# A 16-block attention and mixture-of-experts kernel on one core: q and the output projection as float32r parts, k stored once and read back three times, and new places for all steps

## The reference, cut to what matters

```python
def xattn(q, ctx, w_q, w_kv, w_concat):          # 16 heads of 16, one k and one v shared by all heads
    qh = (q @ w_q).reshape(B, L, 16, 16)
    k, v = split(ctx @ w_kv)
    p = softmax(qh k^T / 4)                       # per block of 128 rows
    return (p v).reshape(B, L, 256) @ w_concat
x = x + xattn(layernorm(x), ctx, ...)
a = layer_norm(layernorm(x)) * nw + nb            # 2048 rows
expert, place = top-1 gate of a, 8 experts, 256 places each
moe = gate * (gelu(a[expert rows] @ W1[e] + b1) @ W2[e] + b2)       # 256 -> 1024 -> 256
res = gelu(a @ R1 + rb1) @ R2 + rb2               # a dense layer of the same shape for all rows
out = x' + coef0 * res + coef1 * moe              # x' = layernorm(x)
```

## Time and profile before

| | us |
|---|---|
| median of 3 runs | 365.86 (365.32 to 366.06) |
| the profiled execution: its own time | 366.06 |
| its span in the profile | 364.3 |
| PE busy | 323.8, 89% of the span |
| DVE, ACT, POOL busy | 228.4, 242.6, 159.8 |
| TensorE's mean granted clock | 0.936 of full |

### The profile page before, as it was taken

One profiled execution on the slowest core, in us unless ns is written; L12 is line 12 of the kernel. 1 busy time (PEld: TensorE's weight loads), 2 busy tenths in 40 slices (PEclk: granted clock), 3 DMA queues, 4 the chain that ended last, 5 costly groups with the idle time before them and its releaser, 6 DMA issues.

```text
span 364.3 us, 7025 instructions
## 1 busy us (share of the span) xinstructions
PE 323.8 (89%) x2514; PEld 280.4 (77%) x2514; DVE 228.4 (63%) x577; ACT 242.6 (67%) x439; POOL 159.8 (44%) x219
## 2 busy tenths in 40 slices
PE   3765887998999999899999989998899999999990
PEld 2543543877897798698798776898899999999990
DVE  4225546985576676576675765465577987788630
ACT  3222277694287588388587476687699999999650
POOL 4222124426986575655654652638003332133222
PEclk9955589996999999999999999999899999999996
DMA  6395756625105505503405301941489888971122
GB/s 186 117 251 160 226 151 175 183 65 161 52 30 180 138 1 173 131 4 122 121 8 166 75 17 38 337 161 40 139 260 318 235 251 266 211 235 21 19 25 29
DMA packets 52490, 49.87 MB, mean 137 GB/s; under 512 B 6684, under 2 KB 49640, under 8 KB 52456
## 3 DMA queue, kind: packets, MB, share of 16 engines
q1 hardware_dynamic: 49384, 45.22, 41.8%
q0 software_dynamic: 3072, 4.21, 6.2%
HBM read 33.65 MB, written 15.63 MB: 135 GB/s over the span
## 4 chain that ended last, share of the span: by engine, by line
PE 73%; DMA 6%; DVE 6%; ACT 5%; POOL 4%; issue 3%; SPq 2%; POOLq 0%; DVEq 0%
PE ubank L678 21%; PE mbank L678 9%; PE mbank L848 8%; PE mbank L849 8%; PE mbank L850 8%; PE mbank L673 4%; PE pbank L765 4%; PE sbank L733 4%; PE sbank L755 3%; DMA qstack<-dram_q 3%; PE pbank L774 1%; PE mbank L707 1%; DVE smax L1073 1%; DMA wq_raw<-in_L_xattn_w_q 1%; ACT h L983 1%
## 5 line engine op out<-in xcount | busy, mean ns | idle before, releaser
L983 ACT ACTIVATE h<-ubank,vecT 128x256 f32<-128x256 f32 x128 | 53.4, 468 | 15.1 <-PE ubank L678 15.0
L646 POOL DMA_INDIRECT out_rows<-yrow,rowid x16 | 27.9, 1744 | 76.0 <-DVE yrow L1218 75.3
L848 PE MATMUL mbank<-w2rh,hh 128*128 128x256 f32 x192 | 60.1, 313 | 0.6 <-DVE hl L1196 0.4
L1196 DVE TENSOR_TENSOR hl<-h,hh 128x512 fp32r<-128x512 f32 x64 | 44.1, 692 | 20.8 <-ACT hh L864 20.3
L1073 DVE TENSOR_REDUCE smax<-sbank 128x4 f32<-128x512 f32 x64 | 42.3, 685 | 22.9 <-PE sbank L733 21.1
L850 PE MATMUL mbank<-w2rh,hl 128*128 128x256 f32 x192 | 55.1, 287 | 0.0
L920 ACT ACTIVATE p<-sbank 128x512 f32<-128x512 f32 x64 | 35.0, 593 | 19.1 <-PE sbank L755 19.1
L849 PE MATMUL mbank<-w2rl,hh 128*128 128x256 f32 x160 | 46.3, 289 | 0.0
L864 ACT ACTIVATE hh<-h 128x512 fp32r<-128x512 f32 x64 | 40.4, 632 | 2.0
L678 PE MATMUL ubank<-aoh,w1rh 128*128 128x256 f32 x192 | 40.7, 293 | 0.0
L848 PEld LDWEIGHTS mbank<-w2rh,hh 128*128 128x128 f32 x192 | 37.9, 197 | 2.5 <-DVE hl L1196 0.8
(11 more groups left out here) (159 smaller groups left out, 767.9 us busy)
## 6 DMA issues: line engine op xcount, KB each, us to landing
qstack<-dram_q SPq DMA_DIRECT2D x16, 384.0 KB, 4.5
w1e<-in_L_ffn_inter_w SPq DMA_DIRECT2D x6, 1024.0 KB, 7.9
w2e<-in_L_ffn_output_w SPq DMA_DIRECT2D x6, 1024.0 KB, 8.6
dram_q<-qpart SPq DMA_DIRECT2D x8, 384.0 KB, 2.6
dispatched<-zrow SPq DMA_DIRECT2D x4, 516.0 KB, 6.3
drow<-dispatched SPq DMA_DIRECT2D x8, 258.0 KB, 4.4
xs<-in_x SPq DMA_DIRECT2D x8, 256.0 KB, 3.0
ctxs<-in_ctx SPq DMA_DIRECT2D x8, 256.0 KB, 3.1
```

What stands on the lines that cost most here:

```text
L646: pool.indirect_dma_start(out=out[:, :], in_=yrow[:, e % 2, t, :], in_offset=None, compute_op=ALU.add, out_offset=bass.IndirectOffsetOnAxi ...
L848: nc.tensor.matmul(b[:, 0:D], hi, wh, start=(f == 0), stop=False)
L983: nc.scalar.activation(h[:, n % 2, f, :], place["up", n, c][:, j, :], ACT.Gelu_apprx_tanh, bias=vecT[:, col:col + 1]).then_inc(sem("gelu_d ...
L1196: V.tensor_tensor(hl[:, n % 2, 2 * c:2 * c + 2, :], a, hh[:, n % 2, 2 * c:2 * c + 2, :].bitcast(f32), ALU.subtract)\
```

## The change

Four things. First, q and proj are computed from float32r parts: ACT's copies write the h part (`wqh`, `xTh`, `wch`, `oTh`), new DVE subtractions write the rest (`wq_split` and `wc_split` once, `x_rest` and `o_rest` once per unit), and each product of 4 float32 matmuls becomes one of 12 float32r matmuls of the same 128x256 shape. PE's `q` and `proj` wait for the DVE subtraction instead of the ACT copy, and the PSUM banks of `xT` and `oT` come free at the subtraction. Second, w_concat is copied and subtracted too (a new ACT step `wc`). Third, `k_spill` writes k's three parts once, in two transfers instead of six, and `gather` reads them back in three instead of one. Fourth, every number of the step tables is new, so the order on each engine changes.

```diff
-    dram_k = nc.dram_tensor("dram_k", [2, REP, DH, UT], bf16).ap()
+    dram_k = nc.dram_tensor("dram_k", [2, 3, DH, UT], bf16).ap()
...
-    PERIOD = 32.1
-    OWN = [0.0, 16.2, 46.34, 78.48]
+    PERIOD = 32.7
+    OWN = [0.0, 15.68, 46.19, 78.99]
...
-        "period": 25.67, "up": [-10.08, -3.74, -1.57, -0.51],
+        "period": 29.05, "up": [-14.74, -10.87, -9.9, -8.88],
...
+    for kind in ("wqs", "wc"):
+        add(LOADS[kind][0], kind, 0)
...
-                     "core", "low", "gate", "loc"):
+                     "core", "low", "gate", "loc", "xrest", "orest"):
...
-        xT = sb("xT", [P, KC, UT], f32, att)
+        xTh = sb("xTh", [P, KC, UT], f32r, att)
+        xTl = sb("xTl", [P, KC, UT], f32r, att)
...
-        wq = sb("wq", [P, KC, D], f32, att)
+        wqh = sb("wqh", [P, KC, D], f32r, att)
+        wql = sb("wql", [P, KC, D], f32r, att)
...
+        wch = sb("wch", [P, KC, D], f32r, att)
+        wcl = sb("wcl", [P, KC, D], f32r, att)
...
-        oT_s = sb("oT", [P, KC, UT], f32, att)
+        oTh = sb("oTh", [P, KC, UT], f32r, att)
+        oTl = sb("oTl", [P, KC, UT], f32r, att)
...
-            "ctxT": ("ctx_copied", lambda u: u + 1), "xT": ("x_copied", lambda u: u + 1),
+            "ctxT": ("ctx_copied", lambda u: u + 1), "xT": ("x_low", lambda u: u + 1),
...
-            "oT": ("oT_copied", lambda u: u + 1), "proj": ("x1_ready", lambda u: u + 1),
+            "oT": ("oT_low", lambda u: u + 1), "proj": ("x1_ready", lambda u: u + 1),
...
-                        sp.wait_ge(sem(f"k_spill{r}"), 3 * T * 16 * U // 2)
+                        sp.wait_ge(sem(f"k_spill{r}"), T * 16 * U // 2)
...
-                    sp.wait_ge(sem(f"stack_in{r}"), 16 * (u // 2))
-                row = 0
-                for parts in (3, 2, 1):
-                    for t in range(T):
-                        sp.dma_start(dram_k[r, row:row + parts, :, t * P:(t + 1) * P].rearrange("a d x -> d a x"),
-                                     kpart[64 * t:64 * t + DH, r, 0:parts, :]).then_inc(sem(f"k_spill{r}"), 16)
-                    row += parts
+                    sp.wait_ge(sem(f"stack_in{r}"), 3 * 16 * (u // 2))
+                for t in range(T):
+                    sp.dma_start(dram_k[r, :, :, t * P:(t + 1) * P].rearrange("a d x -> d a x"),
+                                 kpart[64 * t:64 * t + DH, r, :, :]).then_inc(sem(f"k_spill{r}"), 16)
...
-                    sp.wait_ge(sem(f"k_spill{r}"), 3 * T * 16 * (u // 2 + 1))
-                    sp.dma_start(kstack[0:KS, r, :], dram_k[r].rearrange("a d t -> (a d) t")).then_inc(sem(f"stack_in{r}"), 16)
+                    sp.wait_ge(sem(f"k_spill{r}"), T * 16 * (u // 2 + 1))
+                    row = 0
+                    for parts in (3, 2, 1):
+                        sp.dma_start(kstack[row:row + parts * DH, r, :], dram_k[r, 0:parts].rearrange("a d t -> (a d) t"))\
+                          .then_inc(sem(f"stack_in{r}"), 16)
+                        row += parts * DH
...
             def k_parts(u):
...
-                    pool.wait_ge(sem(f"k_spill{u % 2}"), 3 * T * 16 * (u // 2))
+                    pool.wait_ge(sem(f"k_spill{u % 2}"), T * 16 * (u // 2))
...
             def q(u):
...
-                    pe.wait_ge(sem("wq_ready"), KC)
+                    pe.wait_ge(sem("wq_low"), KC)
...
-                pe.wait_ge(sem("x_copied"), u + 1)
+                pe.wait_ge(sem("x_low"), u + 1)
+                xh, xl = chunks(xTh), chunks(xTl)
...
-                    last = product(b[:, m * UT:(m + 1) * UT], chunks(wq, slice(m * P, (m + 1) * P)), chunks(xT))
+                    wh, wl = chunks(wqh, slice(m * P, (m + 1) * P)), chunks(wql, slice(m * P, (m + 1) * P))
+                    last = product(b[:, m * UT:(m + 1) * UT], wh + wh + wl, xh + xl + xh)
...
             def score_max(u, g):
...
-                    pe.wait_ge(sem(f"stack_in{r}"), 16 * (u // 2 + 1))
+                    pe.wait_ge(sem(f"stack_in{r}"), 3 * 16 * (u // 2 + 1))
...
             def proj(u):
...
-                    pe.wait_ge(sem("wc_in"), 16)
+                    pe.wait_ge(sem("wc_low"), 1)
...
-                pe.wait_ge(sem("oT_copied"), u + 1)
+                pe.wait_ge(sem("oT_low"), u + 1)
+                wh, wl = chunks(wch), chunks(wcl)
...
-                    last = product(b[:, t * D:(t + 1) * D], chunks(oT_s, slice(t * P, (t + 1) * P)), chunks(wc))
+                    oh, ol = chunks(oTh, slice(t * P, (t + 1) * P)), chunks(oTl, slice(t * P, (t + 1) * P))
+                    last = product(b[:, t * D:(t + 1) * D], oh + ol + oh, wh + wh + wl)
...
-                    copy(wq[:, kc, :].rearrange("p (m d h) -> p m d h", m=KC, d=DH),
-                         wq_raw[:, kc, :].rearrange("p (h m d) -> p m d h", m=KC, d=DH)).then_inc(sem("wq_ready"), 1)
+                    copy(wqh[:, kc, :].rearrange("p (m d h) -> p m d h", m=KC, d=DH),
+                         wq_raw[:, kc, :].rearrange("p (h m d) -> p m d h", m=KC, d=DH)).then_inc(sem("wq_high"), 1)
...
-                copy(xT[:, :, :], two(place["xT", u])).then_inc(sem("x_copied"), 1)
+                copy(xTh[:, :, :], two(place["xT", u])).then_inc(sem("x_copied"), 1)
...
-                copy(oT_s[:, :, :], two(place["oT", u])).then_inc(sem("oT_copied"), 1)
+                copy(oTh[:, :, :], two(place["oT", u])).then_inc(sem("oT_copied"), 1)
...
+            def wc_high(u):
+                act.wait_ge(sem("wc_in"), 16)
+                copy(wch[:, :, :], wc[:, :, :]).then_inc(sem("wc_high"), 1)
...
-            calls = {"small": small, "ctxT": ctx_copy, "xT": x_copy, "kv": kv_copy, "q": q_first, "qmid": q_second, "M": max_rows, "B": scores_T,
+            calls = {"small": small, "wc": wc_high, "ctxT": ctx_copy, "xT": x_copy, "kv": kv_copy, "q": q_first, "qmid": q_second, "M": max_rows, "B": scores_T,
...
             def vectors():
...
+            def wq_split(u):
+                for kc in range(KC):
+                    dve.wait_ge(sem("wq_high"), kc + 1)
+                    V.tensor_tensor(wql[:, kc, :].rearrange("p (m d h) -> p m d h", m=KC, d=DH),
+                                    wq_raw[:, kc, :].rearrange("p (h m d) -> p m d h", m=KC, d=DH),
+                                    wqh[:, kc, :].rearrange("p (m d h) -> p m d h", m=KC, d=DH).bitcast(f32), ALU.subtract)\
+                        .then_inc(sem("wq_low"), 1)
+            def wc_split(u):
+                dve.wait_ge(sem("wc_high"), 1)
+                V.tensor_tensor(wcl[:, :, :], wc[:, :, :], wch[:, :, :].bitcast(f32), ALU.subtract)\
+                    .then_inc(sem("wc_low"), 1)
+            def x_rest(u):
+                dve.wait_ge(sem("x_copied"), u + 1)
+                V.tensor_tensor(xTl[:, :, :], two(place["xT", u]), xTh[:, :, :].bitcast(f32), ALU.subtract)\
+                    .then_inc(sem("x_low"), 1)
+            def o_rest(u):
+                dve.wait_ge(sem("oT_copied"), u + 1)
+                V.tensor_tensor(oTl[:, :, :], two(place["oT", u]), oTh[:, :, :].bitcast(f32), ALU.subtract)\
+                    .then_inc(sem("oT_low"), 1)
...
-            calls = {"small": small, "vec": vectors, "ln1": ln1, "xn": norm_x, "qrest": q_rest, "qlast": q_last, "vt": vt, "A": score_max, "M": max_rows, "o": o,
+            calls = {"small": small, "wqs": wq_split, "wc": wc_split, "xrest": x_rest, "orest": o_rest, "vec": vectors, "ln1": ln1, "xn": norm_x, "qrest": q_rest, "qlast": q_last, "vt": vt, "A": score_max, "M": max_rows, "o": o,
...
```

More of the change, by code:

```diff
@@ L63, in xattn_moe_ffn_kernel @@
     AT0 = {
[L64 to L65 removed]
[3 rows of a table removed]
[L69 to L71 removed]
+        "xrest": [-79.89], "orest": [19.81], "load": [-32.19], "ln1": [-125.61], "xn": [-123.15],
[4 rows of a table added]
@@ L72, in xattn_moe_ffn_kernel @@
+        "core": [32.76], "low": [32.49], "gate": [41.98], "loc": [48.15], "gw": [-46.57], "bias": [-177.43],
+        "up": [20.5, 22.17, 23.58, 24.94], "down": [3.17, 5.11, 5.22, 13.16, 15.6, 25.57, 26.22, 27.56],
+        "kspill": [-47.93], "qspill": [-51.47, -43.01, -33.53], "gather": [-25.57, -25.56],
     }
     AT1 = {
-        "load": [-98.66], "ln1": [-94.96], "xn": [-68.04], "ctxT": [-46.31], "xT": [-37.5], "kv": [-44.49],
-        "q": [-39.39], "qrest": [-34.12], "qmid": [-32.1], "qlast": [-41.45], "vt": [-43.31],
[3 rows of a table removed]
@@ L92, in xattn_moe_ffn_kernel @@
+        "gate": [35.99], "loc": [40.66], "gw": [-54.78], "bias": [-3.74], "up": [22.28, 24.26, 26.21, 26.75],
+        "down": [-6.02, -5.4, -4.54, -3.48, 3.43, 4.34, 6.12, 8.02], "kspill": [-38.52],
+        "qspill": [-41.57, -36.52, -35.49], "gather": [-25.02, -20.81],
     }
@@ L94, in xattn_moe_ffn_kernel @@
     LAG_PE = {
-        "core": [-1.39], "gate": [0.0], "loc": [1.29], "A": [-0.29], "B": [1.61], "PV": [1.13], "part": [-2.69],
-        "up": [-0.17], "down": [0.8], "oT": [2.13], "proj": [1.8], "M": [-0.86], "q": [2.69], "kv": [1.3],
-        "vt": [1.37], "xT": [-0.48], "ctxT": [-0.24], "ein": [-3.06], "vec": [-0.08],
```

(13 more changed lines are left out.)

36 lines of the change are left out of this document (19 added, 17 removed), and 21 rows, old and new, of tables (AT, AT0, AT1).

## The result

| | before | changed |
|---|---|---|
| median of the runs, us | 365.96 (4 runs, 365.32 to 366.36) | 361.40 (4 runs, 360.00 to 362.55) |
| ratio to before, 95% interval | 1 | 0.9887 (0.9856 to 0.9918) |
| profiled execution: time, span, us | 366.06, 364.3 | 360.63, 358.9 |

The change takes 4.6 us, 1.1%. The forecast was 359.3 (354.5 to 365.0): the sign is right, the time lies in the range, and the gain is 2.0 us smaller than forecast. That is the smaller part of what there is to learn, because the gain came from other places than the sum had it.

The account below looks back on a forecast made before the run. PE was taken as the bound from 100 us through the experts, with transfers, DVE and PE taking turns at the start. Terms -3.9 - 0.5 - 1.7 - 1.5 - 1.0 + 2.0 = -6.6 us gave 359.3 us for the median, range 354.5 to 365.0.

Parts of the forecast that it names:

- (A): Whole kernel: the sum of terms holds as it stands, 356.5 to 361.5 us; chance 46%.
- Products, -3.9: q and proj where PE is the bound: 14 float32r products save 0.28 us each, 3.9 us in all.
- New waits, +2.0: q and proj wait for ACT's copy and DVE's rest: 0.3 us charged for each of 7 units, +2.0 us.
- The cover is just used up: At q: 3.0 us on ACT and DVE, 3.4 with hand-overs, against 3.3 us of PE work.
- The start, -0.5: Units 0 and 1: first gather 0.4 us earlier, second unchanged; -0.5 us taken, bounds -3 and +2.
- Unit 7's maxima -1.7: PE's wait of up to 1.7 us for unit 7's nmax transfer goes, covered by 30 matmuls; -1.7 us.
- the turn -1.5: Unit 7's core transpose to first expert's rows: chain starts earlier, oT wait covered, six down matmuls moved; -1.5 us.
- the gathers -1.0: PE's waits for A's stack: k spill ends sooner on SP, 1.0 of 1.8 us saved.
- (B): New order gives nothing net, through another clock dip or waits that only move; 361.5 to 365 us, chance 24%.
- Experts, 0: Experts stage: up chunks between down steps change nothing where PE is busy 99.7%; 11.8 us each as before.
- (D): DVE's rests come late, each of 14 products waiting 0.9 us beyond its cover; 369.9 us, slower; chance 11%.
- (C): The start gains its bound, 2.5 us more: 356.8 us, down to 353.5 with fewer new waits; chance 14%.

Follow-up runs that it names:

- no_rests: The changed kernel without the 16 DVE subtractions of x and oT, the middle matmuls reading the high part again; 361.01 us, ratio 0.9847 to the kernel before.
- rests_twice: The changed kernel with each of the 16 subtractions of x and oT done twice; 373.02 us, ratio 1.0165 to the kernel before.
- k_undone: The changed kernel with k transfers as before, six out and one back; 366.04 us, ratio 0.9975 to the kernel before.
- order_only: The kernel before with only the new step tables, float32 products and six k transfers kept; 365.33 us, ratio 0.9975 to the kernel before.
- after_again: The changed kernel unedited, run again on the second set's chip; 362.49 us, ratio 0.9885 to the kernel before.
- after_third: The changed kernel unedited, run once more on the third set's chip; 362.52 us, ratio 0.9876 to the kernel before.
- products_order_before: The changed kernel with the step tables of before, rests put into DVE's order by hand; 370.76 us, ratio 1.0086 to the kernel before.

## Why the prediction was right, and where it was not

The time was right; the way to it was not. The forecast had 359.3 and its central rival (A) 356.5 to 361.5, and 361.4 lies inside both ranges. The start was wrong by 1 to 2 us and the named waits by about 4, with opposite signs, and that they cancelled as far as they did was luck.

**Products, -3.9.** Right in kind, a little too large: 0.25 us each over the steady units where the rows gave 0.28, so 3.5 for 14. (One q taken by its starts saves 0.29; where the rest goes is open.) PE's busy time fell by 4.7 us, not by 6. At half rate a product went from 3.73 to 2.92 us, 0.8 saved of the "up to 1.2".

**New waits, +2.0.** Near in sum, wrong in place. The entries for xTl and oTl are 1.9 us, of which 0.8 stood before as a wait for ACT's copy, so 1.1 are new (no_rests: 1.5 in time). They stand at unit 1, not 0.3 in each steady unit. "The cover is just used up" is nearly what rests_twice shows.

**The start, -0.5.** This is one step that failed: A of unit 0 came 3.4 us earlier, A of unit 1 2.6. Counted from the first q, so without the luck of w_q's load, A of unit 1 gained 1.7 to 2.4 us in three executions, most of the bound of -3. The sum cancelled issues against issues (two loads and two kstack issues against the freed time). It should have asked what SP waits for: the added issues fell into the landing time of the q spill, which itself had moved ahead by 3 us. And "nothing for the second gather" missed that unit 1's gather is queued behind unit 0's nmax, which the new DVE order sends out earlier. The price of the w_concat and w_q subtractions and of the rest at the first q, all taken as covered, was not measured by itself.

**Unit 7's maxima -1.7, the turn -1.5, the gathers -1.0.** This is where the forecast gain of 4.2 us was lost. The named waits did go (nmax at unit 7 from 1.7 us to none, the wait for the oT copy gone, the "issue" waits no longer in the list). The time did not: from q of unit 7 to the first expert's rows the lead grows by 0.9 us, of which the three products in it (q of unit 7, two projections) explain 0.75. So of the 3.2 us forecast for unit 7's maxima and the turn, about 0.1 is left. Before, PE stood idle 6.3 us of these 68.1, after 5.8 of 67.2. In that stretch the changed kernel waits 1.2 us for o_rows, 0.6 for smax and 0.6 for ao, which before had no entries. The prediction priced an order by the waits it removes and gave its new ones no term, except those for the rests. That is the second failed step and the larger one, and its rival (B), "the waits of 1.7 and 1.5 only move", is what happened, without a further dip of the clock. Of the gathers, k_undone and order_only show that the new k transfers do remove a wait of 1.5 us at unit 2; what the steady units gained by the wait of 1.2 that went, they lost to o_rows, smax and qres. The start covered part of it.

**Experts, 0.** Right in the steps of 11.8 us. Whether a half-clock stretch falls on the first expert varies: it was there in after_again (clock 0.73 in 254 to 258 us, 10.5 us from the first expert's rows to the second's) and not in the execution above nor in after_third (9.0 us in both).

**Rivals.** (D), the rests late on DVE, was a near thing: products_order_before is just that, at +3.2 us. It turned there at a mean wait of 6.9 / 16 = 0.4 us per product, of which 0.3 were new, sooner than the 0.6 named. In part this is because the gain at the start is missing in that order; 2.2 us of the loss are open. (C), the start at its bound, came nearly true for the start; (B) for the turn. The time of (A) was met by their sum, not by its own working.

## What to carry to other kernels

Changes that share a chain have no price each: here only the three together brought over 1%, and two of them together once cost 0.9%. A wait that an added instruction causes is a matter of cover, and cover is measured by a kernel that has the instruction twice and one that has it not: here +10.5 and -1.5 us. Where a transfer queue is the chain, count its idle time and what it stands for, not its issues; an issue put into a landing time cost nothing here, and the shorter queue helped only up to the next thing that it waited for in order. When an order is replaced as a whole, the waits it removes are no estimate of its gain: charge it new ones of about the same size. Here 4.2 us of named waits went, and beyond the products the turn gained 0.1 us and three steady units lost 0.9.

## What the hardware showed that was not expected

The granted clock in the records does not always tell the rate of the matmuls. In after_again the row reads 1.00 from 15 to 46 us where the execution shown above reads 0.5, and the matmuls last the same. Stretches of the one and of the other:

```profile
30.00:40.00 10.00, 6.54 (x41) 1.00 0.62 142
```

```profile
30.00:40.00 10.00, 6.88 (x43) 0.50 0.60 148
```

```profile
34.71 0.59 PE L744 MATMUL sbank<-kstack,qstack 96*128 96x128 bf16 x4 [2.36 <-DMA qstack<-dram_q]
```

```profile
34.41 0.59 PE L744 MATMUL sbank<-kstack,qstack 96*128 96x128 bf16 x4 [2.02 <-DMA qstack<-dram_q]
```

Four A matmuls take 0.59 us in both, against 0.40 at full rate later on. In all executions the row says 0.99 or 1.00 for the first 15 us too, while the first q goes at 0.21 us a matmul, the pace of the earlier trace rows. Where the clock matters, the pace of a known matmul is the surer reading.

The same kernel spread over 1 us on one chip, in 4 runs, and over 3.4 to 6.6 on three others, in 14 to 35 runs (before: 365.3 to 366.4, and at the widest 363.3 to 369.9). In the traces the first differences stand in the load of w_q, 3.2 to 4.6 us, on which the whole chain of the start hangs. The half-clock stretch at the first expert is another: 1.5 us between executions of the changed kernel. With effects of 1%, only comparisons on the same chip, by ratio, held together.
